# A mixture-of-experts layer on one Trainium2 core: the first expert bias moves from a TensorE product to a VectorE addition

## The chip, the core and the metric

The kernel runs on one core of a Trainium2 chip. The core has a matrix engine (TensorE, "PE" in the profile, with "PEld" for its weight loads), a vector engine (VectorE, "DVE"), a scalar engine (ScalarE, "ACT"), GpSimd ("POOL") and a queue engine (SyncE, "SP") that issues transfers. Each engine takes its instructions in the order in which they are written, and the engines wait for each other on semaphores. The metric is the time of one execution in microseconds (us), as the median of several runs.

## What is computed

The reference is cross-attention followed by a routed feed-forward layer, both with a residual. Its second part is what the change touches:

```python
x_norm = x / maximum(norm(x), eps); c_norm = ...          # routing scores of 8 experts
gates = _top_k_softmax(cos_scores + route_scores, 2)      # two experts per token
h = gelu(einsum('bsd,edh->bseh', x, w1) + b1, approximate=False)
expert_out = einsum('bseh,ehd->bsed', h, w2) + b2
out = einsum('bse,bsed->bsd', gates, expert_out)
```

There are 16 x 224 = 3584 tokens of 512 numbers, 8 experts, `w1` of 512 x 256 and `w2` of 256 x 512 for each expert, all in float32. `b1` has 8 x 256 numbers and `b2` has 8 x 512. Neither is zero.

## The kernel before

The whole program is one function, `expert_phase`, with one block of instructions per engine. It has three stages.

**Attention** runs over 64 groups (16 batches of 4 groups of heads). For each group `g` every engine has a hand-written order (`first`, `second`, `third`, `fourth`), and `after(g)` in each block adds work at certain groups. At the end of this stage the first bias is prepared. SP loads `b1` as a 128 x 16 tile `b1_s`; PE transposes it in `after(GROUPS - 1)` to 16 x 128 in PSUM; ACT writes its rounded part `b1_th` (line 944) and DVE the rest `b1_tl` (line 1308). GpSimd fills `ones_r` with ones and `b1_hl` with zeros (lines 682 and 683). SP then copies `b1_th` into row 0 and `b1_tl` into row 1 of `b1_hl` (lines 508 and 510), before it issues the last loads of expert weights (line 496). ACT waits for both copies (`b1_both`) before it starts to split the expert weights (`w_part`, line 938).

**Routing** picks two experts per token, builds tables that say which token stands in which slot, and pads each expert's list to whole tiles of 128 slots. SP broadcasts `b2` to `b2_all` on all partitions (line 546) and stores the gates to device memory (line 550). GpSimd waits for the tables and then begins to gather.

**The expert stage** handles 63 tiles of 128 slots, one after another. Float32 products are made as three products of rounded and remaining parts (`h` and `l`). For tile `i`:

- GpSimd gathers the 128 rows to `xg` (`gather`, line 751).
- PE transposes them in four pieces to PSUM (`fold_x`, line 1966).
- ACT copies the rounded part (`x_high`, line 1075) and DVE subtracts to get the rest (`x_low`, line 1550), both to `xTs`.
- PE makes the first layer into `HP` (`up`): first one product of `ones_r` and `b1_hl` for the bias (line 1974), then twelve of 256 columns (lines 1976 to 1978).
- ACT applies the activation from PSUM to `hid` in SBUF (`gelu`, line 1082).
- PE transposes `hid` in two pieces (`fold_h`, line 1986); ACT and DVE split it again (`h_high`, line 1088, and `h_low`, line 1555).
- PE makes the second layer, six products of 512 columns (`down`, lines 1995 to 1997).
- DVE adds `b2` on the way out of PSUM (`y_bias`, line 1566); ACT scales by the gate (`y_scale`, line 1095); GpSimd adds the rows to the output (`add_rows`, line 759).

The order of each engine in loop iteration `i` is what ties the tiles together:

- PE: `fold_x(i+2)`, read the expert's number, `up(i+1)`, `down(i)`, `fold_h(i+1)`
- ACT: `x_high(i+2)`, `gelu(i+1)`, `h_high(i+1)`, `y_scale(i)`
- DVE: `x_low(i+2)`, `y_bias(i)`, read the expert's number, `h_low(i+1)`

The expert's number is read from SBUF to a register by the engine's sequencer (`value_load`, called in `expert_of`; lines 1560 and 2001). All buffers between the engines are two deep.

Of the kernel before, what the change touches and what calls it, by code (L numbers as in the profile page):

```python
# [142 lines left out]
def expert_phase(nc, x1_d, w1, b1, w2, b2, centroids, w_route, ident_d, gates_dram, out):  # L143
    x, ctxT, wqT, bq, wkT, bk, wvT, bv, woT, bo, ident, x1 = SCRATCH["attention"]
    with ExitStack() as es:
# [69 lines left out]
        w1_h, w1_l = in_a("w1_h", [P, E, DC, DE], F32R), in_a("w1_l", [P, E, DC, DE], F32R)  # L215
        b1_hl, ones_r = in_a("b1_hl", [P, E, DE], F32R), in_a("ones_r", [P, P], F32R)
        b1_s, lane = in_a("b1_s", [P, 2 * E]), in_a("lane", [P, 1])
# [20 lines left out]
        in_q, end_q = region(q_own_at)  # L238
        b1_th, b1_tl = in_q("b1_th", [2 * E, P], F32R), in_q("b1_tl", [2 * E, P], F32R)
        assert end_q[0] <= q_own_at + 2 * NQ * 4  # L240
# [72 lines left out]
        made, zeroed, masks = sem("made"), sem("zeroed"), sem("masks")  # L313
        b1_hi, b1_both = sem("b1_hi"), sem("b1_both")
        gate_out, need_done, safe = sem("gate_out"), sem("need_done"), sem("safe")
# [16 lines left out]
        x1v = out.rearrange("(b t p) d -> b p t d", t=QT, p=QP)  # L332
        ctxv = ctxT.rearrange("b (c p) n -> b c p n", p=P)

        raw_k = pr[:].rearrange("p a b c n -> p (a b c n)")[:, 0:CC * D]
# [55 lines left out]
        with nc.Block() as block:  # L391

            @block.sync
            def _(sp):
# [103 lines left out]
                for g in range(-2, GROUPS + LAST):  # L498
                    t, b = g % NG, g // NG
                    if g == GROUPS - NG:  # L500
                        load_res(B - 1)
                    if g == GROUPS - 1:
                        sp.wait_ge(s_full, 12 * (GROUPS - 1))
                        load_pieces(E, E + 2)
                    if g == GROUPS:
                        sp.wait_ge(zeroed, 1)
                        sp.wait_ge(b1_hi, 1)
                        sp.dma_start(b1_hl[0:1, :, :].bitcast(F32), b1_th[:, :].bitcast(F32)).then_inc(b1_both, 16)
                        wait_free(sp, "b1", 0)
                        sp.dma_start(b1_hl[1:2, :, :].bitcast(F32), b1_tl[:, :].bitcast(F32)).then_inc(b1_both, 16)  # L510
                        sp.wait_ge(s_full, 12 * GROUPS)
                        load_pieces(E + 2, 2 * E)
                    if t == 0:
                        stack_k(g + 1)
                        spread_q(g + 2)
                        if 1 <= b - 1 < B - 1:
                            load_res(b - 1)
                        stack_q(g + 1)
                        put_max(g + 1)
                    elif t == 1:  # L520
                        stack_k(g + 1)
                        stack_q(g + 1)
                        spread_q(g + 2)
                        put_max(g + 1)
                    elif t == 2:
                        stack_q(g + 1)
                        if b + 2 < B:
                            load_x(b + 2)
                        stack_k(g + 1)
                        spread_q(g + 2)  # L530
                        put_max(g + 1)
                        store_x1(b - 1)
                    elif t == 3:
                        stack_k(g + 1)
                        if b + 2 < B:
                            for c in range(CC):
                                load_ctx(b + 2, c)
                        spread_q(g + 2)
                        stack_q(g + 1)
                        put_max(g + 1)  # L540
                        store_xn(b - 1)
                    if g == GROUPS - 2:
                        sp.dma_start(b1_s[:, :], b1).then_inc(eb_in, 16)
                        load_pieces(0, E)
                wait_full(sp, "O1", B - 1)
                sp.dma_start(b2_all[:, :, :], b2.rearrange("(a e) n -> a e n", a=1).broadcast_to([P, E, D])
                             ).then_inc(b2_in, 16)
# [14 lines left out]
            def _(pool):  # L562
# [111 lines left out]
                def constants():  # L674
# [6 lines left out]
                              allow_small_or_imprecise_dtypes=True).then_inc(made, 1)  # L681
                    pool.memset(ones_r[:, :].bitcast(F32), 1.0).then_inc(made, 1)
                    pool.memset(b1_hl[:, :, :].bitcast(F32), 0.0).then_inc(zeroed, 1)

                def after(g):
# [12 lines left out]
                    pool.memset(going[:, :, :], 1.0).then_inc(made, 1)  # L698
                    pool.wait_ge(made, 7)
                    pool.memset(going[:, :, 0:1], 0.0).then_inc(made, 1)  # L700
# [4 lines left out]
                    pool.tensor_scalar(upper_half[:, :], token[:, :], 0.0, None, ALU.is_ge).then_inc(made, 1)  # L705
                    pool.wait_ge(made, 11)
                    pool.tensor_tensor(out=token16[:, :], in0=token[:, :], in1=upper_half[:, :], op=ALU.add).then_inc(made, 1)
# [55 lines left out]

                pool.wait_ge(zeroed, 3)
                for n in range(YO):
# [16 lines left out]
            def _(act):  # L782
# [157 lines left out]
                def after(g):  # L940
                    if g == GROUPS - 1:
                        wait_full(act, "b1", 0)
                        act.wait_ge(x_full, XU * GROUPS)
                        act.activation(b1_th[:, :], bank_of("b1", 0)[0:2 * E, 0:P], ACT.Copy).then_inc(b1_hi, 1)
                        yT_part(B - 2, 0)
                        yT_part(B - 2, 1)
                    if g == GROUPS:
# [3 lines left out]
                        wait_full(act, "den", GROUPS - 1)  # L951
                        act.wait_ge(b1_both, 32)
                        for n in range(ACT_EARLY):
# [124 lines left out]
                def gelu(i):  # L1078
                    act.wait_ge(h_full, i + 1)
                    if i >= 2:  # L1080
                        act.wait_ge(ht_full, i - 1)
                    act.activation(hid[:, i % 2, :], HP[:, i % 2, 0:DE], ACT.Gelu).then_inc(gelu_done, 1)

# [29 lines left out]
            def _(dve):  # L1113
# [191 lines left out]
                def after(g):  # L1305
                    if g == GROUPS - 1:
                        dve.wait_ge(b1_hi, 1)
                        dve.tensor_tensor(out=b1_tl[:, :], in0=bank_of("b1", 0)[0:2 * E, 0:P], in1=b1_th[:, :],
                                          op=ALU.subtract).then_inc(freed("b1", 0), 1)
                    if g == GROUPS:  # L1310
                        for n in range(4):
                            w_part(n)
                    if g == GROUPS + 2:
                        dve.wait_ge(made, 8)
                        dve.tensor_scalar(behind[:, :], iota[:, :], float(DUMP + 1), lane[:, 0:1], ALU.add,
# [84 lines left out]
                gp, g1, g2 = gap[0:QP, :], gate4[0:QP, :, 0, 0], gate4[0:QP, :, 1, 0]  # L1400
                dve.wait_ge(made, 5)
                wait_free(dve, "lg0", B - 1)
# [24 lines left out]
                dve.wait_ge(gap_exp, 1)  # L1427
                dve.wait_ge(zeroed, 3)
                dve.wait_ge(x1_out, 16 * B)
# [13 lines left out]
                dve.wait_ge(sums_full, 1)  # L1443
                dve.wait_ge(made, 8)
                dve.tensor_tensor_scan(runs.rearrange("p e k -> p (e k)"), going[0:QP].rearrange("p e k -> p (e k)"), sums,
# [48 lines left out]

                dve.wait_ge(made, 12)
                dve.wait_ge(xn_out, 32 * B)
# [62 lines left out]
                def expert_of(i):  # L1559
                    return dve.value_load(which_i[0:1, i:i + 1], min_val=0, max_val=E - 1)  # L1560

                def y_bias(i, e):
                    dve.wait_ge(y_full, i + 1)
# [7 lines left out]
                e = expert_of(0)  # L1571
                x_low(1)
                h_low(0)
                dve.wait_ge(b2_in, 16)
                for i in range(TILES):
                    if i + 2 < TILES:
                        x_low(i + 2)
                    y_bias(i, e)
                    if i + 1 < TILES:
                        e = expert_of(i + 1)  # L1580
                        h_low(i + 1)


            @block.tensor
            def _(pe):
# [383 lines left out]
                def up(i, e):  # L1969
                    pe.wait_ge(xl_done, i + 1)  # L1970
                    if i >= 2:
                        pe.wait_ge(gelu_done, i - 1)
                    h = HP[:, i % 2, 0:DE]
                    pe.matmul(h, ones_r[:, :], b1_hl[:, e, :], start=True, stop=False)
                    for c in range(DC):
                        pe.matmul(h, xTs[:, 0, i % 2, c, :], w1_h[:, e, c, :], start=False, stop=False)  # L1976
                        pe.matmul(h, xTs[:, 0, i % 2, c, :], w1_l[:, e, c, :], start=False, stop=False)  # L1977
# [26 lines left out]
                pe.wait_ge(table_done, 1)  # L2004
                pe.wait_ge(b1_both, 32)
                pe.wait_ge(rest_out, PE_LOW)
# [59 lines left out]
```

## Time and profile before

| | |
|---|---|
| median of 3 runs | 1539.64 us (1538.95 to 1547.55) |
| profiled execution: span | 1544.8 us; the page gives no other time of this execution |
| PE busy / PEld | 1453.1 us (94%) / 1139.7 us (74%) |
| DVE / ACT / POOL | 994.5 us (64%) / 849.7 us (55%) / 1074.5 us (70%) |
| expert stage | from about 1301 us to the end |

Time is counted from the first instruction of the profiled execution. A row of a timeline gives start, duration, engine, line, operation and operands, and in square brackets how long the engine stood idle before it and what ended that. Busy times of PE overlap from one product to the next, so starts, not durations, give its pace. Numbers in the names of buffers are left out, so `b1_hl` stands as `b_hl` and `b2_all` as `b_all`.

### The profile page before, as it was taken

The numbers are of one execution on the slowest core, as the hardware profiler recorded it, in microseconds if no ns is written. First come the engines' busy times: TensorE is split into PE (matmuls) and PEld (weight loads), VectorE is DVE, ScalarE is ACT, GpSimd is POOL, SyncE is SP. The second block draws the span as 40 slices with busy tenths as digits, with TensorE's granted clock in tenths as the row PEclk, the third lists the DMA queues.
The fourth block names the chain that finished last, engine by engine and source line by source line (L and its number), as shares of the span: only waits on it lengthen the run. The fifth ranks groups of instructions, "written<-read, shape, count | busy, mean of one in ns | idle before, by whom it ended". The sixth has DMA issues, their size and how long they took to land.

```text
span 1544.8 us, 34359 instructions
## 1 busy us (share of the span) xinstructions
PE 1453.1 (94%) x11588; PEld 1139.7 (74%) x11588; DVE 994.5 (64%) x1423; ACT 849.7 (55%) x1807; POOL 1074.5 (70%) x917
## 2 busy tenths in 40 slices
PE   3899999999999999999999999999999687999997
PEld 3667777777777777777777777777777455989896
DVE  5576757676767676767666676667676567444443
ACT  4456555565555565656565655555555362555554
POOL 3367777777777777777777777777777642766775
PEclk9999999999999999999999999999999777999999
DMA  5444444454536363535454535353535473777785
GB/s 180 123 108 127 129 132 135 125 142 117 158 101 174 95 172 100 168 101 161 108 156 114 163 97 163 104 164 107 160 95 146 124 270 49 138 142 130 144 142 85
DMA packets 134953, 206.75 MB, mean 134 GB/s; under 512 B 33808, under 2 KB 70832, under 8 KB 134656
## 3 DMA queue, kind: packets, MB, share of 16 engines
q1 hardware_dynamic: 120544, 173.20, 40.9%
q0 software_dynamic: 14240, 31.35, 11.3%
q8 instruction: 100, 1.64, 0.5%
q14 instruction: 69, 0.57, 0.1%
HBM read 64.29 MB, written 38.66 MB: 67 GB/s over the span
## 4 chain that ended last, share of the span: by engine, by line
PE 79%; POOL 8%; DVE 4%; ACT 4%; issue 3%; DMA 1%; SPq 1%; POOLq 0%; ACTq 0%; DVEq 0%
PE M L379 12%; PE S L1725 11%; PE M L381 11%; PE M L380 11%; PE O L1741 9%; POOL psum_p L583 6%; PE M L1702 4%; ACT pr L867 2%; PE M L1759 2%; PE M L1976 2%; PE M L1995 2%; PE M L1977 2%; PE M L1978 2%; PE M L1996 2%; PE M L1997 2%
## 5 line engine op out<-in xcount | busy, mean ns | idle before, releaser
L583 POOL TENSOR_TENSOR psum_p<-psum_p,pr 125x896 f32<-125x896 f32 x254 | 536.5, 2112 | 153.0 <-ACT pr L867 130.3
L867 ACT ACTIVATE pr<-S 125x448 f32<-125x448 f32 x768 | 385.1, 540 | 173.2 <-PE S L1725 157.0
L1170 DVE TENSOR_REDUCE mx_parts<-M 112x2 f32<-112x1024 f32 x256 | 302.7, 1220 | 106.2 <-PE M L1702 106.2
L1725 PEld LDWEIGHTS S<-qst,kst 128*125 128x125 f32 x1536 | 223.7, 189 | 109.8 <-ACT pr L867 57.1
L1725 PE MATMUL S<-qst,kst 128*125 128x224 f32 x1536 | 285.7, 293 | 14.2 <-ACT pr L867 12.4
L580 POOL TENSOR_TENSOR psum_p<-pr 125x896 f32<-125x896 f32 x64 | 135.0, 2109 | 132.4 <-ACT pr L867 132.4
L1741 PE MATMUL O<-pr,v 125*32 125x224 f32 x3072 | 184.0, 361 | 1.9 <-ACT pr L867 1.9
L1174 DVE TENSOR_REDUCE mx_parts<-M 112x4 f32<-112x952 f32 x128 | 141.2, 1145 | 64.0 <-PE M L1702 64.0
L835 ACT ACTIVATE kh_s<-M,bk_s 128x376 fp32r<-128x376 f32 (+1 forms) x128 | 73.5, 574 | 190.9 <-PE M L381 190.9
L379 PE MATMUL M<-ctx_h,wk_h 128*128 128x376 f32 (+1 forms) x384 | 139.6, 364 | 1.0 <-DVE ql_s L1149 0.6
L380 PE MATMUL M<-ctx_l,wk_h 128*128 128x376 f32 (+1 forms) x384 | 132.7, 346 | 0.0
L381 PE MATMUL M<-ctx_h,wk_l 128*128 128x376 f32 (+1 forms) x384 | 131.5, 343 | 0.0
L759 POOL DMA_INDIRECT out<-y_out,table_t x63 | 99.8, 1585 | 40.0 <-ACT y_out L1095 19.2
L1190 DVE RECIPROCAL M<-M 128x224 f32<-128x224 f32 x64 | 100.1, 1564 | 41.6 <-PE M L1759 39.8
L1741 PEld LDWEIGHTS O<-pr,v 125*32 125x32 f32 x3072 | 82.3, 110 | 57.5 <-issue 17.3
L1158 DVE SCALAR_TENSOR_TENSOR kl_s<-M,bk_s,kh_s 128x376 fp32r<-128x376 f32 (+1 forms) x128 | 76.6, 599 | 73.0 <-ACT kh_s L835 73.0
L751 POOL DMA_INDIRECT xg<-rows_d,table_x x63 | 64.0, 1016 | 80.2 <-DVE settled L1544 38.6
L379 PE MATMUL M<-wv_h,ctx_h 128*125 128x512 f32 x288 | 118.5, 411 | 0.0
L381 PE MATMUL M<-wv_h,ctx_l 128*125 128x512 f32 x288 | 113.6, 395 | 0.0
L380 PE MATMUL M<-wv_l,ctx_h 128*125 128x512 f32 x288 | 113.3, 394 | 0.0
L1702 PE MATMUL M<-kh_s,q_own 32*112 32x512 f32 (+1 forms) x1024 | 94.3, 398 | 8.5 <-issue 3.9
L379 PEld LDWEIGHTS M<-ctx_h,wk_h 128*128 128x128 f32 x384 | 76.8, 200 | 15.9 <-issue 8.1
(253 smaller groups left out, 3042.4 us busy)
## 6 DMA issues: line engine op xcount, KB each, us to landing
kst<-kh_s SPq DMA_DIRECT2D x512, 93.8 KB, 2.3
kst<-kl_s SPq DMA_DIRECT2D x256, 93.8 KB, 2.2
ctx_r<-ctxT SPq DMA_DIRECT2D x48, 375.0 KB, 4.2
qst<-qh_s SPq DMA_DIRECT2D x128, 112.0 KB, 3.0
rows_d<-x_res SPq DMA_DIRECT2D x32, 448.0 KB, 4.3
w_l<-w SPq DMA_DIRECT2D x16, 512.0 KB, 7.9
x_ln<-x SPq DMA_DIRECT2D x17, 448.0 KB, 4.7
q_own<-qh_s SPq DMA_DIRECT2D x256, 28.0 KB, 1.9
```

Of the source, the lines that this page charges most:

```text
L379: pe.matmul(out, lhs[0], rhs[0], start=first, stop=False)
L380: pe.matmul(out, lhs[0], rhs[1], start=False, stop=False)
L381: return pe.matmul(out, lhs[1], rhs[0], start=False, stop=last)
L580: pool.tensor_tensor(out=total, in0=tiles[0], in1=tiles[1], op=ALU.add).then_inc(sum_step, 1)
L583: pool.tensor_tensor(out=total, in0=total, in1=tiles[half], op=ALU.add).then_inc(sum_step, 1)
L867: act.activation(pr[0:KP, (3 * g + p) % 2, j, :, :], S[0:KP, n % SB, 0:2 * NQ].rearrange("p (i n) -> p i n", i=2), ACT.Exp).then_inc(exp_d ...
L1170: dve.tensor_reduce(mx_parts[0:QP, pair, u, 0:1], M[0:QP, pair, 0:FIRST_KEYS], AX.X, ALU.max).then_inc(max_done, 1)
L1174: dve.tensor_reduce(mx_parts[0:QP, pair, :, 1], both, AX.X, ALU.max).then_inc(max_done, 1)
L1190: dve.reciprocal(den, den).then_inc(inverted, 1)
L1702: last = pe.matmul(M[0:QP, j, at:at + w], q_own[head, g % 2, QP * qt:QP * (qt + 1)], kh_s[head, g % 2, off:off + w], start=True, stop=True)
L1725: last = pe.matmul(S[0:KP, n % SB, NQ * h:NQ * (h + 1)], kst[:, i, j, o:o + KP], qst[:, i, j, :], start=True, stop=True)
L1741: last = pe.matmul(O[HD * j:HD * (j + 1), 0:NQ], v[0:KP, 2 * p + i, HD * j:HD * (j + 1)], pr[0:KP, (3 * g + p) % 2, j, i, :], start=(p == ...
```

## The change

The bias is no longer multiplied on PE. ACT copies the transposed `b1` to `b1_t` in full float32, SP writes it to device memory and later reads it back with a broadcast to all 128 partitions (`b1_all`, 1 MB). For each tile DVE adds the row of the tile's expert to the sum in PSUM (`h_bias`) and writes `hid`; ACT then applies the activation to `hid` in place. DVE's order becomes `x_low(i+2)`, read the expert's number, `h_bias(i+1)`, `y_bias(i)`, `h_low(i+1)`. The waits for the first layer's result and for the free `hid` move from ACT to DVE. PE waits for `biased` in place of `gelu_done` before it reuses `HP`. The two memsets, the subtraction, the two copies into `b1_hl` and the waits for them go. The counts of `made` and `zeroed` are adapted.

```diff
-        b1_hl, ones_r = in_a("b1_hl", [P, E, DE], F32R), in_a("ones_r", [P, P], F32R)
+        b1_all = in_a("b1_all", [P, E, DE])
...
+        b1_rows = gates_dram.rearrange("a b c -> (a b c)")[0:E * DE].rearrange("(r c) -> r c", c=P)
+        b1_line = gates_dram.rearrange("a b c -> (a b c)")[0:E * DE].rearrange("(a n) -> a n", a=1)
...
-                        sp.wait_ge(zeroed, 1)
-                        sp.wait_ge(b1_hi, 1)
-                        sp.dma_start(b1_hl[0:1, :, :].bitcast(F32), b1_th[:, :].bitcast(F32)).then_inc(b1_both, 16)
                         wait_free(sp, "b1", 0)
-                        sp.dma_start(b1_hl[1:2, :, :].bitcast(F32), b1_tl[:, :].bitcast(F32)).then_inc(b1_both, 16)
+                        sp.dma_start(b1_rows, b1_t[:, :]).then_inc(b1_sent, 16)
...
                 wait_full(sp, "O1", B - 1)
+                sp.wait_ge(b1_sent, 16)
+                sp.dma_start(b1_all[:, :, :].rearrange("p e f -> p (e f)"),
+                             b1_line.broadcast_to([P, E * DE])).then_inc(b1_in, 16)
...
-                    pool.memset(ones_r[:, :].bitcast(F32), 1.0).then_inc(made, 1)
-                    pool.memset(b1_hl[:, :, :].bitcast(F32), 0.0).then_inc(zeroed, 1)
...
-                        act.activation(b1_th[:, :], bank_of("b1", 0)[0:2 * E, 0:P], ACT.Copy).then_inc(b1_hi, 1)
+                        act.activation(b1_t[:, :], bank_of("b1", 0)[0:2 * E, 0:P], ACT.Copy).then_inc(freed("b1", 0), 1)
...
-                        act.wait_ge(b1_both, 32)
...
                 def gelu(i):
-                    act.wait_ge(h_full, i + 1)
-                    if i >= 2:
-                        act.wait_ge(ht_full, i - 1)
-                    act.activation(hid[:, i % 2, :], HP[:, i % 2, 0:DE], ACT.Gelu).then_inc(gelu_done, 1)
+                    act.wait_ge(biased, i + 1)
+                    act.activation(hid[:, i % 2, :], hid[:, i % 2, :], ACT.Gelu).then_inc(gelu_done, 1)
...
-                    if g == GROUPS - 1:
-                        dve.wait_ge(b1_hi, 1)
-                        dve.tensor_tensor(out=b1_tl[:, :], in0=bank_of("b1", 0)[0:2 * E, 0:P], in1=b1_th[:, :],
-                                          op=ALU.subtract).then_inc(freed("b1", 0), 1)
...
+                def h_bias(i, e):
+                    dve.wait_ge(h_full, i + 1)
+                    if i >= 2:
+                        dve.wait_ge(ht_full, i - 1)
+                    dve.tensor_tensor(out=hid[:, i % 2, :], in0=HP[:, i % 2, 0:DE], in1=b1_all[:, e, :],
+                                      op=ALU.add).then_inc(biased, 1)
...
                 x_low(1)
+                dve.wait_ge(b1_in, 16)
+                h_bias(0, e)
                 h_low(0)
                 dve.wait_ge(b2_in, 16)
                 for i in range(TILES):
                     if i + 2 < TILES:
                         x_low(i + 2)
+                    if i + 1 < TILES:
+                        after = expert_of(i + 1)
+                        h_bias(i + 1, after)
                     y_bias(i, e)
                     if i + 1 < TILES:
-                        e = expert_of(i + 1)
                         h_low(i + 1)
+                        e = after
...
                     if i >= 2:
-                        pe.wait_ge(gelu_done, i - 1)
+                        pe.wait_ge(biased, i - 1)
                     h = HP[:, i % 2, 0:DE]
-                    pe.matmul(h, ones_r[:, :], b1_hl[:, e, :], start=True, stop=False)
                     for c in range(DC):
-                        pe.matmul(h, xTs[:, 0, i % 2, c, :], w1_h[:, e, c, :], start=False, stop=False)
+                        pe.matmul(h, xTs[:, 0, i % 2, c, :], w1_h[:, e, c, :], start=c == 0, stop=False)
...
-                pe.wait_ge(b1_both, 32)
```

## Rows read from the trace of the kernel before

**Rows 1.** Chain of waits, 1306 to 1535 us: shares by engine, tile and line.
```profile
by line: PE M L1976 13.1%; PE M L1977 12.9%; PE M L1978 12.9%; PE M L1995 12.6%; PE M L1996 12.6%; PE M L1997 12.6%; PE S L1966 11.6%; PE M L1974 4.4%; PE O L1986 3.1%; PE M L1986 3.0%; issue 0.8%; DVE y_raw L1566 0.1%; DVEq L1560 0.1%; DVE
```
**Rows 2.** Groups by line, 1306 to 1530 us: count, busy us, mean ns, idle before.
```profile
L1974 PE MATMUL M<-b_hl,ones_r 128*128 x61 | 22.4, 368 | 1.7 <-issue 1.5
L1555 DVE TENSOR_TENSOR hTs<-O,hTs 128x256 fp32r<-128x256 f32 x31 | 13.2, 425 | 5.6 <-ACT hTs L1088 2.9 <-issue 2.6
L1555 DVE TENSOR_TENSOR hTs<-M,hTs 128x256 fp32r<-128x256 f32 x30 | 12.7, 425 | 2.2 <-issue 2.0
...
L1974 PEld LDWEIGHTS M<-b_hl,ones_r 128*128 128x128 f32 x61 | 11.5, 189 | 4.1 <-issue 3.6
```
**Rows 3.** Timeline of one ordinary tile, 1441.8 to 1446.2 us.
```profile
1441.88 0.37 PEld L1986 LDWEIGHTS M<-id_s,hid 128*128 128x128 f32 x2
...
1442.42 0.69 DVE L1566 TENSOR_TENSOR y_raw<-M,b_all 128x512 f32<-128x512 f32 x1 [1.03 <-PE M L1997]
...
1442.66 0.19 PEld L1974 LDWEIGHTS M<-b_hl,ones_r 128*128 128x128 f32 x1
1442.69 0.36 PE L1974 MATMUL M<-b_hl,ones_r 128*128 x1
1442.77 0.19 PEld L1976 LDWEIGHTS M<-w_h,xTs 128*128 128x128 f32 x1
1442.89 0.29 PE L1976 MATMUL M<-w_h,xTs 128*128 x1
...
1443.08 0.42 DVE L1555 TENSOR_TENSOR hTs<-M,hTs 128x256 fp32r<-128x256 f32 x1
...
1443.15 0.72 ACT L1095 ACTIVATE y_out<-y_raw,xg 128x512 f32<-128x512 f32 x1 [0.23 <-DVE y_raw L1566]
...
1443.78 0.58 ACT L1075 ACTIVATE xTs<-S 128x512 fp32r<-128x512 f32 x1
...
1444.39 0.69 DVE L1550 TENSOR_TENSOR xTs<-S,xTs 128x512 fp32r<-128x512 f32 x1 [0.88 <-ACT xTs L1075]
1444.53 0.38 ACT L1082 ACTIVATE hid<-M 128x256 f32<-128x256 f32 x1 [0.17 <-PE M L1978]
...
1445.49 0.38 PEld L1986 LDWEIGHTS O<-id_s,hid 128*128 128x128 f32 x2
```
**Rows 4.** Timeline of a tile whose activation came late, 1341.6 to 1343.7 us.
```profile
1341.95 0.39 ACT L1082 ACTIVATE hid<-M 128x256 f32<-128x256 f32 x1 [0.85 <-PE M L1978]
...
1342.38 0.23 PEld L1986 LDWEIGHTS O<-id_s,hid 128*128 128x128 f32 x2 [0.19 <-ACT hid L1082]
...
1343.36 0.19 PEld L1974 LDWEIGHTS M<-b_hl,ones_r 128*128 128x128 f32 x1 [0.31 <-issue]
```
**Rows 5.** All of line 1974: min/median/max ns, first and last start.
```profile
L1974 PEld LDWEIGHTS M<-b_hl,ones_r x63: 186/190/289, 1302.5 to 1531.0; 128*128 128x128 f32 x63
```
**Rows 6.** Line 1560, DVE's sequencer reading the expert's number; columns as before.
```profile
L1560 DVEq TENSOR_LOAD <-which_i x63: 299/306/957, 1301.4 to 1534.4; - x63
L1560 DVEq FUSED_REGOPS  x63: 190/190/216, 1302.0 to 1534.8; - x63
```
**Rows 7.** Line 1566, the sequencer's step for an address that depends on the expert.
```profile
L1566 DVEq FUSED_REGOPS  x63: 57/57/65, 1310.1 to 1537.3; - x63
```
**Rows 8.** Line 2001, PE's sequencer reading the same number.
```profile
L2001 PEldq TENSOR_LOAD <-which_i x63: 297/466/812, 1301.5 to 1530.2; - x63
```
**Rows 9.** Who waited for whom, 1240 to 1302 us: us in total, times, longest.
```profile
POOL xg L751 <- DVE settled L1544: 38.6, 1, 38.6
```
**Rows 10.** Line 938, ACT's splitting of expert weights: idle before it.
```profile
  DMA b_hl<-b_tl: 0.7, 1
```
**Rows 11.** Timeline of the transfers' issue and the tables' end, 1240 to 1302 us.
```profile
1265.74 0.92 SPq L546 DMA_DIRECT2D b_all<-b  x1
...
1272.76 4.39 SPq L550 DMA_DIRECT2D rows_d<-gate  x2
...
1294.68 0.15 DVE L1544 COPY settled<-ones 128x1 f32<-128x1 f32 x1
```
**Rows 12.** Transfers issued from 1264 to 1302 us: size, median us to landing.
```profile
b_all<-b SPq DMA_DIRECT2D x1, 2048.0 KB, 11.1
...
rows_d<-gate SPq DMA_DIRECT2D x2, 56.0 KB, 10.3
```
**Rows 13.** Busy us of each engine by stretch, granted clock (the column after POOL).
```profile
1224.00:1240.00 16.00, 9.88 (x76) 6.47 (x71) 3.32 (x7) 6.70 (x14) 11.18 (x20) 0.69 0.85 260
1306.00:1530.00 224.00, 222.27 (x1522) 200.30 (x1523) 107.92 (x182) 119.83 (x243) 149.95 (x117) 1.00 0.75 134
```

More of the change, by code:

```diff
@@ L238, in expert_phase @@
         in_q, end_q = region(q_own_at)
-        b1_th, b1_tl = in_q("b1_th", [2 * E, P], F32R), in_q("b1_tl", [2 * E, P], F32R)
+        b1_t = in_q("b1_t", [2 * E, P])
         assert end_q[0] <= q_own_at + 2 * NQ * 4
@@ L313, in expert_phase @@
         made, zeroed, masks = sem("made"), sem("zeroed"), sem("masks")
-        b1_hi, b1_both = sem("b1_hi"), sem("b1_both")
+        b1_sent, b1_in = sem("b1_sent"), sem("b1_in")
+        biased = sem("biased")
         gate_out, need_done, safe = sem("gate_out"), sem("need_done"), sem("safe")
@@ L698, in after @@
                     pool.memset(going[:, :, :], 1.0).then_inc(made, 1)
-                    pool.wait_ge(made, 7)
+                    pool.wait_ge(made, 6)
                     pool.memset(going[:, :, 0:1], 0.0).then_inc(made, 1)
@@ L705, in after @@
                     pool.tensor_scalar(upper_half[:, :], token[:, :], 0.0, None, ALU.is_ge).then_inc(made, 1)
-                    pool.wait_ge(made, 11)
+                    pool.wait_ge(made, 10)
                     pool.tensor_tensor(out=token16[:, :], in0=token[:, :], in1=upper_half[:, :], op=ALU.add).then_inc(made, 1)
@@ L762, in add_rows @@
                                             oob_is_err=False, compute_op=ALU.add).then_inc(added[i % YO], 16)
-                pool.wait_ge(zeroed, 3)
+                pool.wait_ge(zeroed, 2)
                 for n in range(YO):
@@ L1313, in after @@
                     if g == GROUPS + 2:
-                        dve.wait_ge(made, 8)
+                        dve.wait_ge(made, 7)
                         dve.tensor_scalar(behind[:, :], iota[:, :], float(DUMP + 1), lane[:, 0:1], ALU.add,
@@ L1400, in _ @@
                 gp, g1, g2 = gap[0:QP, :], gate4[0:QP, :, 0, 0], gate4[0:QP, :, 1, 0]
-                dve.wait_ge(made, 5)
+                dve.wait_ge(made, 4)
                 wait_free(dve, "lg0", B - 1)
@@ L1427, in _ @@
                 dve.wait_ge(gap_exp, 1)
-                dve.wait_ge(zeroed, 3)
+                dve.wait_ge(zeroed, 2)
                 dve.wait_ge(x1_out, 16 * B)
@@ L1443, in _ @@
                 dve.wait_ge(sums_full, 1)
-                dve.wait_ge(made, 8)
+                dve.wait_ge(made, 7)
                 dve.tensor_tensor_scan(runs.rearrange("p e k -> p (e k)"), going[0:QP].rearrange("p e k -> p (e k)"), sums,
@@ L1493, in find_rows @@
                                       op=ALU.is_equal).then_inc(row_done, 1)
-                dve.wait_ge(made, 12)
+                dve.wait_ge(made, 11)
                 dve.wait_ge(xn_out, 32 * B)
```

## The prediction, made before the changed kernel was run

> **What bounds the kernel now.** I read the chain of waits of the expert stage first, since the change's repeated part lies there. PE's products hold nearly all of it, the bias product 4.4%, and a wait for another engine hardly occurs [rows 1]. So the stage runs at PE's pace, and what matters is how far the other engines are from setting it. The starts of one ordinary tile show that. PE begins to load the transposed `hid` of one tile at 1441.88 and of the next at 1445.49, 3.61 us later [rows 3]. Over the stage, 63 bias products start between 1302.5 and 1531.0, or 228.5 / 62 = 3.686 us each [rows 5]; the surplus over 3.61 is mostly the sequencer of PE being late with the bias product, 1.5 + 3.6 = 5.1 us in all [rows 2].
>
> The same tile shows how the engines depend on each other. DVE's `y_bias` starts at 1442.42, ACT's `y_scale` at 1443.15, and because ACT takes its work in order, `x_high` of a later tile only at 1443.78; `x_low` follows at 1444.39 [rows 3]. The activation starts at 1444.53, beside `x_low`, and ends at 1444.91. PE wants it at 1445.49, so it has 0.58 us to spare. That reserve is what the change spends.
>
> **The change in the expert stage.** It takes the bias product off PE. Weight loads for it and for the first real product start at 1442.66 and 1442.77 [rows 3]: 0.11 us a tile. Were PE alone the bound, that is 62 x 0.11 = 7 us, at most 62 x 0.20 = 12 us by the starts of the two products, 1442.69 and 1442.89 [rows 3].
>
> It puts `h_bias` behind `x_low` on DVE and the activation behind `h_bias`. `h_bias` reads 256 columns from PSUM and 256 from SBUF as `h_low` does, so I price it at 0.425 us [rows 2]. Its start is worked out from two distances. First, the next instruction on DVE starts 0.66 us after one of 0.69 us (1442.42 to 1443.08 [rows 3]). Second, the expert's number must now be read between the two: the sequencer takes 306 ns for the load and 190 ns for the check [rows 6], 57 ns for the address [rows 7] and two waits. The old order had load and check behind `y_bias`, whose 0.66 us contains them, but needed no address right after. I add 0.14 us for address, waits and their gaps: 0.80 us from `x_low` to `h_bias`. The lower bound is 0.66, the upper 0.90.
>
> The activation now reads SBUF. I leave it at 0.38 us: the trace has no such pair.
>
> By the Trainium skill (Perfetto Trace Analysis, Optimizing Scalar/DVE Operations) an ACT instruction on SBUF carries about 93 ns of access overhead against about 51 ns on PSUM. By that the activation would be some 0.04 us longer and the total, estimated from that page, 1 us higher.
>
> Now **the loop through all engines**, from the moment A at which PE starts the last product of `down(i)` (1441.88, when the weight load of `fold_h` starts too):
>
> - A to `y_bias`: 0.54; to `y_scale`: 0.73; to `x_high(i+3)`: 0.63; to `x_low(i+3)`: 0.61 [rows 3]
> - to `h_bias(i+2)`: 0.80
> - to the activation: 0.425 + 0.04 = 0.47
> - to PE's load of `hid` in `fold_h(i+2)`: 0.43, from the late tile, 1341.95 to 1342.38 [rows 4]
>
> The sum is 4.21 us. It ends at `fold_h(i+2)`, one tile after `fold_h(i+1)`, and 4.21 is 0.6 more than the 3.61 between them. So PE will wait there.
>
> How long PE then takes from `fold_h(i+2)` to the last product of `down(i+2)` also changes, because its sequencer no longer runs ahead. In the ordinary tile the first weight load of `up` follows the load of `hid` by 0.78 us (1441.88 to 1442.66 [rows 3]); in the tile where PE had to wait for the activation, by 0.98 us, with 0.31 us of it "issue" (1342.38 to 1343.36 [rows 4]). The register read, stuck behind the wait of `fold_h`, is late. From that weight load to the next `fold_h` are 1445.49 - 1442.66 = 2.83 us, less 0.11 for the bias product: 2.72. Together 0.98 + 2.72 = 3.70 us.
>
> The two paths close a loop in two tiles: 4.21 + 3.70 = 7.91 us, 3.955 us a tile. A gap that is short in one tile is long in the next, and the sum stays. Against 3.686 this is 0.269 us more. The first tile is outside the loop, so 61 x 0.269 = 16.4 us. Late register reads come on top: DVE's cost 2.6 + 2.0 = 4.6 us of idle time ahead of `h_low`, harmless before [rows 2], now on the path, half of it in a loop of two tiles: 2.3 us. PE's 5.1 us are in the 3.686 but not in the 3.70, half again: 2.6 us. The stage: 21.3 us slower.
>
> In place of 306 ns the Trainium skill (DMA: Bandwidth & Descriptors, Latency and other measured facts) gives a floor of about 600 ns for such a register load. The trace disagrees, with 306 ns on DVE and minima of 299 and 297 ns [rows 6, 8]. With that page's figure DVE's part alone would add, as an estimate, 0.3 / 2 x 61 = 9 us.
>
> **Ahead of the stage.** ACT waited 0.7 us for the copies into `b1_hl` before splitting weights [rows 10]; without them it starts that much earlier, while the tables hang on routing behind it. I take 0.3 us off, between 0 and 0.7. The two memsets, 2 us of POOL beside other work, the subtraction of 16 rows and the last weight loads issued earlier by SP cost or bring nothing: POOL sits idle 38.6 us before the first gather [rows 9]. SP gets one store of 8 KB more in place of two copies, and a broadcast of 1 MB ahead of `b2` (issued at 1265.74 [rows 11]). `b2`'s 2 MB took 11.1 us [rows 12], so the broadcast is worth 5.6 us of traffic. What queues behind it: `b2`, first used at about 1310, and the two gate stores, issued from 1272.76 to 1277.15 and 10.3 us to landing [rows 11, 12], so landed by 1287.5 at the latest. Moved by 5.6 us that is 1293.1, still ahead of the tables at 1294.68 [rows 11]. `b1_all` itself lands some 20 us before DVE waits for it. In tile 0, `h_bias` adds 0.47 us and the missing product takes back at most 0.29, the longest of its weight loads [rows 5]: +0.2.
>
> **Sum:** 21.3 - 0.3 + 0.2 = 21 us. The profiled execution would go from a span of 1544.8 to 1566. That span lies 5.2 us above the median of the runs, which I take as constant: 1539.6 + 21 = **1561 us**, 1.4% slower.
>
> **The range of this case.** At the good end `h_bias` starts 0.66 after `x_low` and `up` follows by 0.88: (4.07 + 3.60) / 2 = 3.835, 9 us, and late reads are absorbed: 1549. At the bad end `h_bias` starts after 0.90 and PE's register read takes its median of 466 ns [rows 8] where the late tile had the quick kind, near 0.31: (4.31 + 3.86) / 2 = 4.085, 24 us, with 5 for late reads: 1569.
>
> **The rivals.**
>
> 1. *The loop closes, but PE's sequencer keeps ahead.* The 0.98 us rests on one tile. If `up` follows `fold_h` at the engine's own pace, 0.78 - 0.11, PE's part is 3.39 and the period between 3.73 and 3.80: 3 to 7 us slower, 1542 to 1547. Against it: the "issue" of 0.31 in that tile and the order of PE's instructions.
> 2. *The other side: the reserve suffices and only PE's relief shows.* It would need `h_bias` to be done by 1445.0 in the ordinary tile, so before or beside `x_low`. For it: PE bounds the stage now, and DVE is busy for half of it. Against it: `x_low` is written ahead of `h_bias` and itself waits for `x_high`. It decides at 0.58 us: if activation and bias come no later than that, the gain is 7 to 12 us, 1528 to 1533.
> 3. *PE's clock falls.* The granted clock is 1.00 with PE busy 222 of 224 us and 0.69 where it is busy 9.88 of 16 us [rows 13]. In my forecast PE does 3.4 us of work in 3.96, between the two. At the lower level (1.2 GHz, against 2.4) its part doubles, to about 7.1, and a tile takes (4.21 + 7.1) / 2 = 5.7 us, 1.7 more; for one tile in ten this is 10 us on top of the forecast, 1571. The Trainium skill (TensorE: Matmul & The Clock Gate, A second HAM failure mode) describes such a fall from frequent short idle gaps between groups of products; no stretch of this trace has such gaps at a steady pace.
> 4. *Traffic.* The broadcast delays the gates beyond the tables. Needs more than 7 us (1287.5 to 1294.68) where I expect 5.6; each further us shifts the stage by one: 1565.
>
> Chances: the forecast 0.62, the first rival 0.18, the second 0.12, the third 0.05, the fourth 0.03. That the product stays or the bias is read wrong isn't a case: both are in the listing.
>
> **The numbers.** A change of 1%, 15.4 us, is about what a measurement of this kernel can tell from none. Slower by over 1% means above 1555.0: four fifths of the forecast's case, and the last two, 0.50 + 0.08 = 0.58. Within 1% are the first two rivals and the rest of the forecast, 0.42, of which I give 0.04 to a gain beyond 1% that I have no mechanism for. The range 1543 to 1572 leaves out the second rival and the tails.
>
> **What the profile will show.** Right: bias products gone, DVE's `hid` rows of 0.42 us starting about 0.8 after `x_low`; PE idle before `fold_h` (line 1986), released by the activation; "issue" ahead of line 1976; a tile at 3.9 to 4.0 us on average, perhaps alternating 3.7 and 4.2; clock 1.00. Wrong: a period under 3.6 with no wait at `fold_h` (second rival); a wait there without "issue" behind it (first rival). The prediction falls if `h_bias` doesn't follow `x_low`, or if something outside the expert stage moves by more than 2 us.

## The result, and the profile after

The changed kernel takes 1572.15 us (median of 4 runs, 1568.53 to 1573.1) against 1541.24 us. The ratio is 1.0195, 95% interval 1.0163 to 1.0227: 25 to 35 us slower. The kernel before has a fourth run here, so its median is 1541.24 and not 1539.64. The forecast was 21 us, and its direction and mechanism held. Its size held less well: 30 us is more than the 29 us of its bad end (24 and 5 for late reads), and 1572.15 lies at the upper edge of its range of 1543 to 1572. The two profiled executions differ by less, 1566.6 - 1544.8 = 21.8 us. One of these was the slowest of its kernel and the other the fastest, and the difference lies in attention, whose code is the same in both: its last exponential starts at 1243.0 us before and 1237.1 after. So I compare the expert stage by its own length, taken from one profiled execution of each kernel. The x64 row of line 1992 gives it as the first to the last weight load of `fold_h` (first and last start):

```profile
L1992 PEld LDWEIGHTS O<-id_s,hid x64: 138/141/145, 1300.6 to 1556.0; 128*128 128x128 f32 x64
...
  ACT hid L1081: 20.4, 36
  issue: 19.4, 41
```

From 1300.6 to 1556.0 are 255.4 us. The 62 distances between tiles, taken from the single records, are 255.2 us, or 4.12 us each, against 227.9 us and 3.68 before: 27.4 us more. The last two rows say what ended PE's idle time ahead of `fold_h`: the activation, 36 times, and 41 times nothing that the profile names. The starts are clearer. In all of the 62 tiles after the first, the load of `fold_h` starts 0.47 us after its activation, as soon as it is done; before, it started 0.96 us after it in the median tile, and under 0.5 us in 6. The idle time then was

```profile
  ACT hid L1082: 2.2, 6
```

The chain of waits of this stage, 1300 to 1560 us, shows the same from the other side [rows 1]:

```profile
by line: issue 14.8%; PE M L1982 11.4%; PE M L2003 7.4%; PE M L2001 7.4%; PE M L2002 7.3%; PE M L1984 7.3%; PE M L1983 7.3%; PE S L1973 6.5%; ACT xTs L1076 4.3%; DVE xTs L1545 4.1%; PE M L1992 4.0%; DVE y_raw L1568 4.0%; PE O L1992 3.4%; AC
```

PE no longer holds it alone: `x_high` (ACT, line 1076), `x_low` (DVE, line 1545) and `y_bias` (line 1568) are on it, and "issue" has grown from 0.8% to 14.8%, some 38 us between the first `fold_h` and the last. The loads and checks of registers on PE and DVE cover only 9 of these. In most of the rest the profile finds no releaser, as for the last row below, though its load comes 0.47 us after the activation like every other. One tile, as the timeline has it (the answer to [rows 3, 4]):

```profile
1440.70 0.23 PEld L1992 LDWEIGHTS O<-id_s,hid 128*128 128x128 f32 x2 [0.19 <-ACT hid L1081]
...
1441.10 0.69 DVE L1568 TENSOR_TENSOR y_raw<-M,b_all 128x512 f32<-128x512 f32 x1 [0.90 <-PE M L2003]
...
1441.67 0.19 PEld L1982 LDWEIGHTS M<-w_h,xTs 128*128 128x128 f32 x1 [0.30 <-issue]
...
1441.82 0.72 ACT L1094 ACTIVATE y_out<-y_raw,xg 128x512 f32<-128x512 f32 x1 [0.23 <-issue]
...
1442.45 0.58 ACT L1076 ACTIVATE xTs<-S 128x512 fp32r<-128x512 f32 x1
...
1443.06 0.69 DVE L1545 TENSOR_TENSOR xTs<-S,xTs 128x512 fp32r<-128x512 f32 x1 [0.94 <-ACT xTs L1076]
...
1444.22 0.42 DVE L1561 TENSOR_TENSOR hid<-M,b_all 128x256 f32<-128x256 f32 x1 [0.47 <-issue]
...
1444.68 0.42 ACT L1081 ACTIVATE hid<-hid 128x256 f32<-128x256 f32 x1 [1.65 <-DVE hid L1561]
...
1445.15 0.20 PEld L1992 LDWEIGHTS M<-id_s,hid 128*128 128x128 f32 x2 [0.83 <-issue]
```

Every step of the forecast's loop is there in order. The first load of `up` follows `fold_h` by 0.97 us (1440.70 to 1441.67) with 0.30 of "issue". But `h_bias` starts 1.16 us after `x_low`, not 0.80, and the row says "issue": DVE's sequencer was reading the expert's number, from 1443.08 to 1443.72. The reads on DVE and PE, and the activation, over all 63 tiles (min/median/max ns; [rows 6, 8]):

```profile
L1555 DVEq TENSOR_LOAD <-which_i x63: 301/552/964, 1295.5 to 1553.1; - x63
```
```profile
L2007 PEldq TENSOR_LOAD <-which_i x63: 297/301/491, 1295.5 to 1552.2; - x63
```
```profile
L1081 ACT ACTIVATE hid<-hid x63: 416/417/420, 1300.1 to 1555.3; 128x256 f32<-128x256 f32 x63
```

DVE's median went from 306 to 552 ns, PE's from 466 to 301. The slow reads have changed engines. Ahead of the stage the broadcast lands in 9.5 us, and the gate stores now take 15.3 us to land where they took 10.3 [rows 12]:

```profile
b_all<-gates_dram SPq DMA_DIRECT2D x1, 1024.0 KB, 9.5
...
rows_d<-gate SPq DMA_DIRECT2D x2, 56.0 KB, 15.3
```

That is 5.0 us later, and nothing waited for it: GpSimd still waits 37.6 us for the tables (38.6 before [rows 9]). The granted clock over 1300 to 1550 us is 1.00, with PE busy 235.31 of 250 us [rows 13]:

```profile
1300.00:1550.00 250.00, 235.31 (x1454) 189.21 (x1455) 132.67 (x242) 117.89 (x243) 149.80 (x116) 1.00 0.69 119
```

### The profile page after: what moved, and what is told of

Its sections match the earlier page's. It is cut to its first block, busy times and chain, and to the rows that moved or that the text cites. A ratio compares the mean times of both kernels' runs of the same rounds, so it can differ in the third digit from the quotient of the medians.

```text
span 1566.6 us, 34293 instructions
## 1 busy us (share of the span) xinstructions
PE 1464.8 (94%) x11525; PEld 1126.2 (72%) x11525; DVE 1020.6 (65%) x1485; ACT 848.2 (54%) x1807; POOL 1077.0 (69%) x915
## 4 chain that ended last, share of the span: by engine, by line
PE 71%; POOL 11%; issue 5%; DVE 5%; ACT 5%; DMA 1%; SPq 1%; DVEq 0%; POOLq 0%; ACTq 0%
PE M L383 11%; PE S L1732 11%; PE M L384 10%; PE M L385 10%; PE O L1748 9%; POOL psum_p L587 8%; PE M L1709 4%; PE M L1766 2%; ACT pr L869 2%; PE M L1982 2%; PE M L1643 1%; PE M L2003 1%; PE M L2001 1%; PE M L2002 1%; PE M L1984 1%
## 5 line engine op out<-in xcount | busy, mean ns | idle before, releaser
L571 POOL TENSOR_TENSOR ctx_l<-ctx_r,ctx_h 128x750 fp32r<-128x750 f32 x48 | 87.9, 1861 | 0.0
```

## The experiments

Theory L, the forecast's: PE, ACT and DVE close a loop every two tiles. One part goes from the last product of `down(i)` over `y_bias`, `y_scale`, `x_high`, `x_low`, `h_bias` and the activation to `fold_h(i+2)`; the other is PE's own way from there to the next `down`. Whatever is taken off one part shows by half in each tile. Theory M was formed on the two traces: a register read that is under way when a transfer of `add_rows` begins is held up, on any engine. The single records of the changed kernel between 1312 and 1530 us show it. Of DVE's 52 reads, 38 end 1.06 to 1.16 us after the first packet of such a transfer, whenever they began; they take 0.35 to 0.96 us, 0.62 on average. The 6 that meet no such moment take 0.34. SP's reads of its own numbers show the same: the 40 that end after the first packet and begin no later than 0.8 us behind it take 0.61 us on average, the 116 others 0.28. Before, it was PE's reads that met that moment.

In the diffs, "..." stands for unchanged lines. Unless said otherwise the base is the changed kernel. Each kernel was timed against the kernel before, and the weight load rows of `fold_h` stand at the end of this section. The profiled executions of experiments 1 to 3 differ in one more thing: their granted clock was 0.5 until 1304.4, 1305.9 and 1306.1 us, so some 3.7 us into the stage, and their first tile takes 5.04, 5.09 and 5.23 us where it takes 3.66 in the changed kernel. Some 1.3 us of each of their stages come from that.

**1. DVE reads one tile ahead.**

```diff
+                after = expert_of(1)
                 for i in range(TILES):
...
-                        after = expert_of(i + 1)
                         h_bias(i + 1, after)
                     y_bias(i, e)
+                    e = after
+                    if i + 2 < TILES:
+                        after = expert_of(i + 2)
                     if i + 1 < TILES:
                         h_low(i + 1)
-                        e = after
```

> The changed kernel, with DVE reading the expert's number one tile ahead, behind y_bias. Loop theory (DVE, ACT and PE close a loop every two tiles): x_low to h_bias falls from a mean of 1.08 us to 0.66 to 0.70, half of 0.4 us on 61 tiles, 12 us: about 1560 us against 1572. Rival A (PE's sequencer alone sets the pace): no change, 1572. Rival B (DVE simply has too much work): no change, since the read isn't engine work.

Measured: 1555.59 us, ratio 1.0093 (1.0060 to 1.0127). `x_low` to `h_bias` fell from 1.08 to 0.65 us, and the stage from 255.2 to 242.2 us, 13.0 less where 12 were expected. Rivals A and B fall: nothing but the place of a register read on DVE was changed.

**2. The bias ahead of `x_low`.**

```diff
                 for i in range(TILES):
-                    if i + 2 < TILES:
-                        x_low(i + 2)
                     if i + 1 < TILES:
                         after = expert_of(i + 1)
                         h_bias(i + 1, after)
+                    if i + 2 < TILES:
+                        x_low(i + 2)
                     y_bias(i, e)
```

> The changed kernel, with h_bias(i+1) put ahead of x_low(i+2) on DVE, register read still right before it. Loop theory: x_low and x_high leave the path. What is left goes from up through h_bias and the activation to fold_h and PE's late register read: 1.76 us (first weight load of up to its release) + 0.46 + 0.47 + 0.98 = 3.67 us a tile instead of 4.12, so 28 us less: about 1544 us. Rival B (DVE's work or the operand in SBUF costs it, whatever the order): within 5 us of 1572. Rival C (the gain of taking the product off PE appears at once): 1530.

Measured: 1548.91 us, ratio 1.0044 (1.0021 to 1.0067). The stage takes 237.8 us, 17.5 less, not 28. Rivals B and C fall. The median tile is 3.74 us and the mean 3.84; I had expected 3.67. The direction is as expected, the size is missed by over a third, 10.5 us. Some 4.6 of these are missing in the median tile already: `h_bias` starts 1.84 us after the first load of `up` there, not 1.76. The rest is the mean over the median: that distance is 1.90 us on average, and the load follows `fold_h` by 1.01 us, since PE's read is slow in some tiles (its slowest 830 ns).

**3. PE reads one tile ahead.**

```diff
+                after = expert_of(1)
                 for i in range(TILES):
                     if i + 2 < TILES:
                         fold_x(i + 2)
                     if i + 1 < TILES:
-                        after = expert_of(i + 1)
                         up(i + 1, after)
                     down(i, e)
+                    e = after
+                    if i + 2 < TILES:
+                        after = expert_of(i + 2)
                     if i + 1 < TILES:
                         fold_h(i + 1)
-                        e = after
```

> The changed kernel, with PE reading the expert's number one tile ahead, between down and fold_h. Loop theory: fold_h to the first weight load of up falls from 0.97 us to 0.65, half of 0.32 on 61 tiles, 10 us: about 1562. Rival A (PE's sequencer alone sets the pace): the full 0.32 us a tile, 20 us: 1552. Rival D (the chain over ACT and DVE closes in one tile, PE's part is slack): no change, 1572.

Measured: 1558.63 us, ratio 1.0105 (1.0064 to 1.0146). By the runs that is some 14 us less than the change. By the trace `fold_h` to `up` fell from 0.97 to 0.60 us, but the stage only from 255.2 to 249.2: `y_bias` to `y_scale` grew from 0.81 to 0.93 us, because `y_scale` stands behind `h_high` on ACT and was held by it in 36 tiles, against 24 in the changed kernel. In such tiles a chain over ACT and DVE closes in one tile, so rival D holds for a part of the tiles; as the whole account it falls, since PE's read did matter. Rival A's full 0.32 us a tile, 20 us, came in neither measure. The 10 us expected lie between the two measures; this experiment alone doesn't fix the size.

**4. No bias product, in the kernel before.**

```diff
-                    pe.matmul(h, ones_r[:, :], b1_hl[:, e, :], start=True, stop=False)
                     for c in range(DC):
-                        pe.matmul(h, xTs[:, 0, i % 2, c, :], w1_h[:, e, c, :], start=False, stop=False)
+                        pe.matmul(h, xTs[:, 0, i % 2, c, :], w1_h[:, e, c, :], start=c == 0, stop=False)
```

> The kernel before without the bias product of the first layer, and so without that bias; all else as before, its preparation too. It shows what PE's relief alone is worth. Forecast's term: 0.11 us a tile, 7 us, at most 12: 1529 to 1534 against 1541. Rival (PE isn't the bound before, or the sequencer's register read takes the place of the product): 1539 to 1541.

Measured: 1538.4 us, ratio 0.9974 (0.9954 to 0.9993), 1 to 7 us, short of the 7 to 12 expected. The median tile is 3.494 us against 3.610, just the 0.11 forecast, but the mean falls only from 3.676 to 3.616, 3.7 us in all. So without the product something else takes back half of its time; that it is PE's register read is shown by experiment 9.

**5. Rows written, not added.**

```diff
-                                            oob_is_err=False, compute_op=ALU.add).then_inc(added[i % YO], 16)
+                                            oob_is_err=False).then_inc(added[i % YO], 16)
```

> The changed kernel, with the expert rows written over the output instead of added to it (the sum of the layer's parts is left out); same transfers in number and size. DVE's register read takes 0.54 us on average in the changed kernel and took 0.37 before; in both traces the slow reads are those under way when the row-adding transfer begins. Theory M (the start of that transfer, which reads memory before it writes, holds register reads up): the reads fall to about 0.31 us, half of 0.23 on 61 tiles, 7 us: 1565. Rival N (PE's products or DVE's own subtraction, under way at the same time, slow the read): it stays at 0.54 and the time at 1572. Rival O (any start of a transfer from SBUF does it): the read stays above 0.45.

Measured: 1562.37 us, ratio 1.0148 (1.0105 to 1.0191). The reads of DVE, 63 as before:

```profile
L1555 DVEq TENSOR_LOAD <-which_i x63: 299/304/554, 1299.5 to 1548.4; - x63
```

Their mean fell from 0.540 to 0.309 us, and the stage by 8.8 us to 246.4; 7 were expected, and `y_scale`, 0.07 us less behind `y_bias`, gives some 2 more. Engines and order are the same and the reads run beside the same products and subtractions, so N falls. The mean tile, 3.975 us, is close to the 3.955 that the forecast had for quick reads, and two tiles together take 7.93 us in the median, where the forecast's loop has 7.91.

O isn't excluded. The rows and bytes are the same, but the plain write is another transfer: in the traces it has packets of 4 KB, 3156 of them between 1312 and 1530 us, where the adding one has 6208 of 2 KB, and its queue is busy for about half as long (1310 to 1530 us: packets, MB, share of 16 engines; first the changed kernel, then this one):

```profile
q0 software_dynamic: 11832, 26.83, 70.4%
```
```profile
q0 software_dynamic: 8720, 27.47, 38.3%
```

And DVE's reads began 0.61 us or more after its first packet, so none of them met its start. SP's did: 26 that end after that packet and begin no later than 0.3 us behind it took 0.45 us on average, up to 0.74, against 0.27 for its 170 others. A plain write holds reads up as well, for a shorter time. What the experiment shows is that the hold comes from the row transfer and what it costs, not that the adding is needed for it.

**6. Bias first, both reads ahead** (the edits of 2 on DVE, with the reads placed as in 1 and 3).

> The changed kernel with h_bias(i+1) ahead of x_low(i+2), and with both PE and DVE reading the expert's number one tile ahead. Loop theory: up to up is then 1.76 + 0.46 + 0.47 + 0.65 = 3.34 us, under PE's own 3.49; PE is the bound again, without its bias product and without its late reads: 3.49 to 3.55 us a tile, 35 to 39 us less than the change: 1533 to 1537, faster than the kernel before by 6 to 10 us. Rival (the second addition on DVE costs something in any order): no better than the kernel before, 1541 to 1544.

Measured: 1529.69 us, ratio 0.9937 (0.9916 to 0.9959): faster than both kernels, 6 to 13 us under the kernel before. The stage takes 216.6 us, 3.493 a tile, and its chain is PE's again, with PE busy all of the time and the clock at 1.00:

```profile
1310.00:1500.00 190.00, 190.00 (x1306) 172.03 (x1305) 115.25 (x218) 109.42 (x218) 138.34 (x109) 1.00 0.79 145
```

DVE makes the second addition in every tile and it costs nothing that shows: experiment 9, without any bias, takes 217.5 us. In the timeline `h_bias` waits for PE (line 1986 here), and in this tile the activation is done before PE comes to `fold_h`:

```profile
1401.33 0.43 DVE L1561 TENSOR_TENSOR hid<-M,b_all 128x256 f32<-128x256 f32 x1 [0.34 <-PE M L1986]
1401.67 0.68 DVE L1545 TENSOR_TENSOR xTs<-S,xTs 128x512 fp32r<-128x512 f32 x1
1401.79 0.42 ACT L1081 ACTIVATE hid<-hid 128x256 f32<-128x256 f32 x1 [0.61 <-DVE hid L1561]
1402.36 0.37 PEld L1994 LDWEIGHTS M<-id_s,hid 128*128 128x128 f32 x2
```

The activation ends at 1402.21, 0.15 us before PE's load. That isn't the common case: in 59 of 62 tiles the load follows the activation by 0.47 us, so it waited for it. PE's products run on meanwhile, and the wait stays hidden, but there is no reserve left in this order.

**7. The kernel before, PE reads ahead** (the edit of 3).

> The kernel before with one edit: PE reads the expert's number one tile ahead. Without its bias product alone (the fourth experiment) the median tile fell by 0.116 us but the mean only by 0.06, as if PE's sequencer took back the rest. Theory (PE's late register reads are the surplus of the mean, 3.676, over the median, 3.61): the mean falls to 3.62 us, 3 to 4 us in all, 1538 to 1540. Rival (other stalls of PE's instruction stream make the surplus): no change, 1541 to 1543.

Measured: 1540.16 us, ratio 1.0002 (0.9978 to 1.0027). The mean tile fell from 3.676 to 3.609 us, as expected, 4.1 us in the trace. The runs don't show it: their interval holds no gain at all and ends at one of 3.4 us.

**8. The change, both reads ahead** (the edits of 1 and 3).

> The changed kernel with both reads one tile ahead and DVE's order kept. Loop theory: 0.54 + 0.73 + 0.62 + 0.615 + 0.65 + 0.45 + 0.47 = 4.08 us by ACT and DVE, 0.61 + 2.70 = 3.31 by PE, together 7.39, 3.69 us a tile: 229 to 232 us for the stage where the change takes 255, so 23 to 26 us less: 1546 to 1549, still slower than before. Rival A (only PE's sequencer was at fault): 1535. Rival D (a chain over ACT and DVE that closes in one tile): no better than the first experiment's 1556.

Measured: 1543.54 us, ratio 1.0028 (0.9995 to 1.0061). The stage takes 227.3 us, 3.667 a tile against 3.69 by the sum (229 to 232 expected). This is the best check of the two-tile loop: all its terms were known, and it is neither the 3.31 us of PE's way alone nor the 3.91 of the first experiment, so rivals A and D fall. PE still waits for the activation in all 62 tiles. With the forecast's order on DVE and both reads ahead, the stage is as long as before the change (227.9), and 3.5 us longer than the kernel before with PE's read ahead (223.8, experiment 7).

**9. Experiment 4 with PE reading ahead.**

> The kernel before without the bias product (that bias is left out), and with PE reading the expert's number one tile ahead. In the fourth experiment the median tile fell by 0.116 us and the mean by 0.06. Theory (PE's late reads took the difference): mean and median both at 3.49 us, 216 to 218 us for the stage, 1530 to 1533. Rival (other stalls): the mean stays above 3.58.

Measured: 1532.04 us, ratio 0.9926 (0.9901 to 0.9951). Mean 3.509 and median 3.486 us, 217.5 us for the stage. The difference between mean and median in experiment 4 was PE's read. This is what PE's relief is worth once nothing takes its place; experiment 6 has all of it with the bias added.

**10. Bias first, only PE reads ahead** (the edits of 2 and 3).

> The changed kernel with h_bias ahead of x_low and only PE reading ahead; DVE reads the expert's number right before h_bias, while it waits for the first layer. Theory (only a read on the path costs): as with both reads ahead, 3.49 to 3.52 us a tile, 1529 to 1533. Rival (a late read on DVE costs in any place): 3.6 us or more, 1537 and up.

Measured: 1534.42 us, ratio 0.9943 (0.9916 to 0.9971). Neither theory is clean: the median tile is 3.481 us, as in experiment 6, but the mean 3.581, and the stage 222.0 us, 5.4 more. The surplus sits in 11 tiles, in which `h_bias` starts 2.3 to 2.7 us after the first load of `up` and not 1.84, 6.6 us in all. It isn't DVE's read: in each of them the read was over 0.95 us after that load at the latest. `h_bias` was waiting for the first layer's last product, whose signal came 0.5 to 0.8 us later than usual, as here, while PE went on at its ordinary pace:

```profile
1467.93 0.19 PEld L1982 LDWEIGHTS M<-w_h,xTs 128*128 128x128 f32 x1
...
1470.46 0.42 DVE L1561 TENSOR_TENSOR hid<-M,b_all 128x256 f32<-128x256 f32 x1 [1.75 <-PE M L1984]
```

Experiment 6 has no such tile, and why the signal is late here isn't shown. The runs of 6 and 10 don't differ.

The weight loads of `fold_h` in experiments 1 to 4, 6 and 8 (last less first start of these is the stage):

```profile
L1994 PEld LDWEIGHTS O<-id_s,hid x64: 137/140/224, 1300.8 to 1543.2; 128*128 128x128 f32 x64
```
```profile
L1992 PEld LDWEIGHTS O<-id_s,hid x64: 137/139/229, 1302.1 to 1540.1; 128*128 128x128 f32 x64
```
```profile
L1992 PEld LDWEIGHTS O<-id_s,hid x64: 138/141/226, 1302.4 to 1551.7; 128*128 128x128 f32 x64
```
```profile
L1985 PEld LDWEIGHTS O<-id_s,hid x64: 138/139/143, 1300.9 to 1525.3; 128*128 128x128 f32 x64
```
```profile
L1994 PEld LDWEIGHTS O<-id_s,hid x64: 138/139/144, 1300.5 to 1517.2; 128*128 128x128 f32 x64
```
```profile
L1994 PEld LDWEIGHTS O<-id_s,hid x64: 138/140/143, 1303.2 to 1530.7; 128*128 128x128 f32 x64
```

## Why the prediction was right, and where its sizes were off

**The reserve of 0.58 us is spent, and the loop of two tiles closes.** Shown by the wait at `fold_h` in every tile, by tiles that alternate between about 3.75 and 4.18 us once the reads are quick (experiment 5; in the changed kernel itself they range from 3.61 to 4.74), and by experiments 1, 5 and 8, whose stage came within 2.5 us of half the change in their terms. Experiment 3 came 5 us short of it, 4 of which are the growth of `y_scale`.

**Its terms.** Means over the tiles of the changed kernel, with the forecast in brackets: last product of `down` to `y_bias` 0.54 (0.54), to `y_scale` 0.81 (0.73), to `x_high` 0.62 (0.63), to `x_low` 0.61 (0.61), to `h_bias` 1.08 (0.80), to the activation 0.46 (0.47), to `fold_h` 0.47 (0.43). That is 4.59 us (4.21). PE's way: 0.97 to `up` (0.98) and 2.70 on to the last product of the next `down` (2.72), 3.67 (3.70). Half of 8.26 is 4.13; measured 4.12 (3.955, or 4.035 with the forecast's late reads).

**The mis-sized term is the register read on DVE.** I took 0.80 us from the median of 306 ns, and allowed 2.3 us in all for slow reads by the idle time that they had caused. But I read that price off a place in the tile where no transfer began. The change moved the read from behind `y_bias` to behind `x_low`, and there it meets the start of the row-adding transfer: 0.540 us on average instead of 0.306 when quick, half of 0.234 on 61 tiles, 7.1 us. The 0.80 us itself was good: with the quick reads of experiment 5 the distance is 0.84. Experiment 5 gave 8.8 back by changing only that transfer. In return the 2.6 us that I kept for PE's late reads went away, as PE's read moved off that moment (mean 0.306 us).

**The activation's operand.** I left it at 0.38 us; it takes 0.417 from SBUF where it took 0.384 from PSUM, half of 0.033 on 62 tiles or 1 us over the stage. The Trainium skill (Perfetto Trace Analysis, Optimizing Scalar/DVE Operations) gives some 0.04 us for this move; the trace agrees.

**`y_scale`** comes 0.08 us later than after `y_bias` alone, on average: behind a late `fold_h` it waits for `h_high` on its own engine, in 24 of the 62 tiles. The forecast's sum has no such link. Half of it is 2.6 us. In those tiles the loop closes in one tile and not in two: from `fold_h` over `h_high` to `y_scale` are 0.76 us, and with 0.62, 0.61, 1.08, 0.46 and 0.47 behind it that is 4.0 us, near the 4.12 measured. With quick reads, 0.82 in place of 1.08, it is 3.74 us, which is just what the short tiles of experiment 5 take. No run takes this link out, by `y_scale` ahead of `h_high`.

**Ahead of the stage** I took 0.3 us off. From the last exponential to the first `fold_h` are 62.96 us before and 63.48 after, and 62.0 to 63.7 in the ten experiments: too near to tell. ACT does start to split weights without the wait (no idle time is listed ahead of line 940 now), and the gates take 5.0 us longer to land where I expected 5.6, with no one waiting.

**The rivals.** PE's sequencer didn't keep ahead (first rival): 0.97 us on average and never under 0.84, as the one late tile had shown. The second rival's condition, `h_bias` beside or before `x_low`, is what experiments 2 and 6 made true. In experiment 2 no gain came, 1548.91 us, since PE's read was still late; in experiment 6, with both reads ahead, it was 6 to 13 us. That this meets the 7 to 12 forecast is in part luck: by the traces 4.1 us of it are PE's read ahead, which the kernel before could have had too (experiment 7, 223.8 us), and the rest is 7.2 us. The granted clock stayed at 1.00 in the stage, and the traffic stayed hidden.

**What stays open.** The whole gap by the runs, 30 us, against 27.4 in the stage and 0.5 ahead of it lies within the interval. Why the start of a row transfer holds register reads up isn't shown, nor whether the adding, the number of packets or their longer times make the hold longer than that of a plain write.

## What to carry to other kernels

Work that is moved to an engine with spare time is priced by its place in that engine's order and not by the engine's load: with both reads ahead, the same addition behind `x_low` made the stage 227.3 us, and ahead of `x_low` 216.6, where it is 217.5 without any bias. Where two-deep buffers tie engines together, sum the whole loop and divide by the tiles that it spans; the sum from rows of the old trace was within 4% of the new period. These 4% are 10 us here, over a third of the effect: a register read is priced where it will stand, not where it stood. And read a register one step ahead of its use: a late read hides behind work only until that work is removed.

## What the runs showed of the hardware that I had not expected

A sequencer's read of one number from SBUF takes 0.30 us when undisturbed on DVE and PE, and 0.27 on SP. One that meets the first microsecond of a transfer that adds rows into device memory mostly ends only 1.06 to 1.16 us after that transfer's first packet, so 0.35 to 0.96 us after its own start; at 1443.7 us DVE's read and SP's end together, after 0.64 and 0.94 us. At the start of a plain write SP's reads took 0.45 us on average, at most 0.74. The floor of about 600 ns that the Trainium skill (DMA: Bandwidth & Descriptors, Latency and other measured facts) gives for such a load is twice what an undisturbed one took here, and near only to those that met the transfer. And when PE's instruction stream is held by a wait ahead of the read, the next layer's first weight load comes 0.97 us after the released one (changed kernel); with the read one tile ahead it comes after 0.60 (experiments 3 and 8).
